# Routing stage of a one-core attention + mixture-of-experts kernel: constants, first rows and bias rows fetched during the attention stage, slots placed one iteration sooner, w2 two parts a step

## What is computed

```python
x = x + conv_ref(ln_c(x), w_qkv, b_qkv, rpb, w_proj, b_proj)     # attention ... out @ w_proj.T + b_proj
t = to_tokens(x)
# t + ffn(ln_t(t)):
gate_logits = xf @ Wg + bg
top_w, top_i = top_k(gate_logits, 2); top_w = softmax(top_w)
for e in range(E):
    h = gelu(xf @ W1[e] + b1[e], approximate=False)
    out = out + w_dense[:, e:e + 1] * (h @ W2[e] + b2[e])
```

## Time and profile before

| what | value |
|---|---|
| median of 3 executions | 1350.75 us (1346.7 to 1353.21) |
| the profiled execution | 1352.15 us, span 1350.3 us |
| busy, share of the span | PE 85%, PE weight load 72%, DVE 67%, POOL 55%, ACT 47% |
| last tile of the attention stage done | about 510 us after the span's start |
| first instructions of stage_c | 512.14 us |
| last send of stage_c issued | 685.31 us |
| first instruction of stage_e on POOL | 690.93 us |

### The profile page before, as it was taken

How to read it: one execution, slowest core, us unless ns; L and a number is a source line. 1 busy time by engine, 2 the same in 40 slices (tenths; PEclk the granted TensorE clock), 3 DMA queues, 4 the chain that set the end, 5 groups by cost and what they waited for, 6 DMA issues and landing times. The chain is left out here.

```text
span 1350.3 us, 38316 instructions
## 1 busy us (share of the span) xinstructions
PE 1143.8 (85%) x12145; PEld 967.9 (72%) x12146; DVE 907.0 (67%) x3154; ACT 630.7 (47%) x1305; POOL 737.9 (55%) x792
## 2 busy tenths in 40 slices
PE   2888855889988885998139999999999999999995
PEld 1655635888887884876028888888888888888884
DVE  6666645888888784887326666666666666666662
ACT  2555544888888783765113333333333333333331
POOL 5111123666666560577734666666566665666655
PEclk9899886999999996998569999999999999999998
DMA  6566648776767736999521323332232332323332
GB/s 166 154 210 210 197 152 196 191 186 180 185 179 183 194 115 190 350 356 304 187 75 26 49 47 50 48 48 48 44 52 47 49 48 45 50 48 48 48 49 28
DMA packets 152234, 169.85 MB, mean 126 GB/s; under 512 B 14334, under 2 KB 144014, under 8 KB 151766
## 3 DMA queue, kind: packets, MB, share of 16 engines
q1 hardware_dynamic: 114996, 131.54, 34.4%
q0 software_dynamic: 21920, 29.38, 13.2%
q10 hardware_dynamic: 15250, 8.11, 2.4%
HBM read 108.36 MB, written 65.49 MB: 129 GB/s over the span
## 5 line engine op out<-in xcount | busy, mean ns | idle before, releaser
L1523 ACT ACTIVATE e_gf<-e_ps_h,keep_b 128x256 f32<-128x256 f32 x448 | 211.8, 473 | 414.3 <-PE e_ps_h L1470 414.3
L1470 PE MATMUL e_ps_h<-e_xt,w1s 128*128 128x256 f16 x2688 | 323.2, 275 | 5.1 <-PEq L1462 3.8
L1470 PEld LDWEIGHTS e_ps_h<-e_xt,w1s 128*128 x2688 | 247.8, 98 | 73.5 <-issue 39.2
L1485 PE MATMUL e_ps_y<-w2s,e_g_hi 128*128 x1792 | 296.4, 273 | 0.0
L825 POOL TENSOR_TENSOR b_p<-b_s,b_p 128x392 f16<-128x392 f32 x196 | 182.6, 931 | 119.9 <-DVE b_p L723 116.0
L1485 PE MATMUL e_ps_y<-w2s,e_g_lo 128*128 x896 | 244.4, 273 | 0.0
L1423 POOL DMA_INDIRECT out<-e_y,e_xg x112 | 182.6, 1630 | 78.4 <-POOLq L1420 44.5
L1546 DVE TENSOR_TENSOR e_g_lo<-e_gf,e_g_hi 128x256 f16<-128x256 f32 x448 | 207.1, 462 | 15.5
L1485 PEld LDWEIGHTS e_ps_y<-w2s,e_g_hi 128*128 128x128 f16 x1792 | 172.9, 98 | 19.3
L780 ACT ACTIVATE b_s<-b_s,b_neg_max 128x196 f32<-128x196 f32 x392 | 158.3, 455 | 21.1 <-DVE b_neg_max L704 20.9
L1544 DVE CAST e_g_hi<-e_gf 128x256 f16<-128x256 f32 x448 | 145.7, 325 | 23.3 <-ACT e_gf L1523 23.3
(11 more groups left out here) (142 smaller groups left out, 1652.8 us busy)
## 6 DMA issues: line engine op xcount, KB each, us to landing
b_v<-v_rows SPq DMA_DIRECT2D x196, 99.5 KB
e_xg<-slots SPq DMA_DIRECT2D x56, 273.0 KB, 2.8
b_k<-qk_hi SPq DMA_DIRECT2D x56, 196.0 KB
a_w_in<-in_w SPq DMA_DIRECT2D x16, 512.0 KB, 3.7
c_w_in<-in_w SPq DMA_DIRECT2D x16, 512.0 KB, 9.6
v_rows<-a_v SPq DMA_DIRECT2D x14, 455.0 KB, 6.9
a_x<-in_x SPq DMA_DIRECT2D x14, 448.0 KB, 6.3
qk_hi<-a_o_hi SPq DMA_DIRECT2D x14, 448.0 KB, 4.4
```

The source lines that it names most:

```text
L1470: mm = pe.matmul(ps_h[:, hc % 4, 0:ST], w1s[:, bass.ds(e, 1), w, a:a + 128].rearrange("p a n -> p (a n)"), xt[:, s, :, 2 * p + k, :], star ...
L1485: mm = pe.matmul(ps_y[:, s, h * C:(h + 1) * C], g[:, s, hc, h * 128:(h + 1) * 128], w2s[:, bass.ds(e, 1), w, a:a + C].rearrange("p a n -> ...
L1523: act.activation(gf[:, hc % 4, :], ps_h[:, hc % 4, 0:ST], ACT.Gelu, bias=b1_sb[:, bass.ds(e * HC + hc, 1)], scale=1.0 / WSCALE).then_inc(g ...
```

## The change

- A new function `opening` makes the buffers for constants, weights, bias rows and first rows once, for stage_b and stage_c both. stage_b's SP issues the nine DMAs of constants and weights ahead of the second band, and the first two steps' attention and input rows in the middle of the last band. stage_b's DVE makes the bias rows after its last tile (`projection_bias`).
- In stage_c, `place(i - 1)` is in DVE's iteration i, behind `low_half(i - 1)`; `rank(i - 1)` on PE is ahead of `turn_xn(i)`.
- The w2 parts are two a step in steps 2 to 9 and none elsewhere. On ACT `high_w2` is behind `high_half`, as the last thing of an iteration.
- ACT begins with a square root on the constant `eps`; SP loads the first w2 parts behind the attention rows of steps 2 and 3.

```diff
@@ stage_b, SP
                             sp.wait_ge(v_free, n + 1)
+                            if r_next is None and n == COLS:
+                                for i in range(2):
+                                    sp.dma_start(op["a"][:, i, 0:SIZES[i]], token_rows(attn, i)).then_inc(op["a_in"][i], 16)
+                                    sp.dma_start(op["x"][:, i, 0:SIZES[i]], token_rows(x, i)).then_inc(op["x_in"][i], 16)
...
                 pair(0, 0, 1, QR - HALF)
+                sp.dma_start(op["b_f"][:, :], bproj.to_broadcast([128, C])).then_inc(op["b_ld"], 16)
+                sp.dma_start(op["id"][:, :], ident).then_inc(op["w_ld"], 16)
+                sp.dma_start(op["w_p"][:, :, :], wproj).then_inc(op["w_ld"], 16)
...
@@ stage_b, DVE
+                def projection_bias():
+                    b_f, b_part, b_rows, step = op["b_f"], op["b_part"], op["b_rows"], op["b_step"]
+                    dve.memset(b_rows[96:128, :], 0.0)
+                    dve.memset(op["even"][:, :], 1.0 / 32)
+                    dve.memset(op["eps"][:, :], 1e-5)
+                    dve.wait_ge(op["b_ld"], 16)
+                    for n in range(3):
+                        dve.tensor_copy(b_part[:, :], b_f[:, :]).then_inc(step, 1)
...
                 pair(row_offset(BANDS - 1), False, True)
+                projection_bias()
                 for t in range(COLS):
                     dve.wait_ge(stored[t], 32)
@@ stage_c
-        parts = [[i] if i < STEPS_C - 2 else [2 * i - 12, 2 * i - 11] for i in range(STEPS_C)]
+        parts = [[2 * i - 4, 2 * i - 3] if 2 <= i < 2 + E else [] for i in range(STEPS_C)]
...
-                load_a(0)
-                load_x(0)
-                load_a(1)
-                load_x(1)
-                sp.dma_start(w_g[:, :, :], wg).then_inc(g_ld, 16)
-                for p in range(2):
-                    load_w2(p)
                 for i in range(2):
                     sp.wait_ge(a_tr, i + 1)
                     load_a(i + 2)
+                for p in range(2):
+                    load_w2(p)
@@ stage_c, PE
                     if i + 1 < STEPS_C:
                         project(i + 1)
+                    if i:
+                        rank(i - 1)
                     turn_xn(i)
                     if i + 2 < STEPS_C:
                         turn_attention(i + 2)
-                    if i == 1:
-                        pe.wait_ge(k_in, 80)
-                    if i:
-                        rank(i - 1)
                     gate_logits(i)
@@ stage_c, ACT
-                act.dma_start(id_c[:, :], ident).then_inc(w_ld, 16)
...
-                act.wait_ge(ready, 1)
+                act.activation(sd[:, 0, 0:1], eps[:, :], ACT.Sqrt)
                 take_attention(0)
                 take_attention(1)
                 for i in range(STEPS_C):
                     roots(i)
                     normalise(i)
-                    for p in parts[i]:
-                        high_w2(p)
                     take_xn(i)
                     if i + 2 < STEPS_C:
                         take_attention(i + 2)
                     high_half(i)
+                    for p in parts[i]:
+                        high_w2(p)
@@ stage_c, DVE
-                bias_rows()
-                for i in range(STEPS_C + 2):
+                dve.memset(hot[:, :, :, :].rearrange("p s b e -> p (s b e)").bitcast(F32), 0.0).then_inc(ready, 1)
+                for i in range(STEPS_C + 1):
                     if i < STEPS_C:
                         residual(i)
-                    if i >= 2:
-                        place(i - 2)
-                    if i < STEPS_C:
                         scales(i)
-                    if 1 <= i <= STEPS_C:
+                    if i:
                         choose(i - 1)
                         low_half(i - 1)
+                        place(i - 1)
                     if i < STEPS_C:
                         for p in parts[i]:
                             low_w2(p)
```

More of the change, by code:

```diff
@@ L452, in _, with opening, sb, sem @@
                 step(1, True)
-def stage_b(nc, qk_hi, qk_lo, v_rows, bias, q_mask, k_mask, ident16, attn):
+def opening(nc, c):
+    def sb(name, shape, dt):
+        return c.enter_context(nc.sbuf_tensor("o_" + name, shape, dt))
+    def sem(name):
+        return c.enter_context(nc.semaphore("o_" + name))
+    return {
+        "id": sb("ident", [128, 128], F32),
+        "w_p": sb("w_p", [128, KC, C], F32),
+        "w_g": sb("w_g", [128, KC, E], F32),
+        "b_f": sb("b_f", [128, C], F32),
+        "b_part": sb("b_part", [128, C], BF16),
+        "b_rows": sb("b_rows", [128, C], BF16),
+        "even": sb("even", [128, 128], BF16),
+        "b_g": sb("b_g", [128, E], F32),
+        "eps": sb("eps", [128, 1], F32),
+        "cf": sb("consts", [128, C_CONSTS], F32),
+        "tri": sb("tri", [128, 2, 128], BF16),
+        "tok": sb("tok", [128, TOKENS // 128], I32),
+        "tc": sb("tiles", [1, T_CONSTS], F32),
+        "a": sb("a", [128, 2, GPS, C], F32),
+        "x": sb("x", [128, 2, GPS, C], F32),
+        "w_ld": sem("w_ld"), "b_ld": sem("b_ld"), "g_ld": sem("g_ld"), "k_in": sem("k_in"), "b_step": sem("b_step"),
+        "a_in": [sem(f"a_in{i}") for i in range(2)], "x_in": [sem(f"x_in{i}") for i in range(2)],
+    }
+def token_rows(t, i):
+    at = sum(SIZES[:i])
+    return t[at * 128:(at + SIZES[i]) * 128, :].rearrange("(g p) c -> p g c", p=128)
+def stage_b(nc, qk_hi, qk_lo, v_rows, bias, q_mask, k_mask, ident16, attn, x, wproj, bproj, wg, bg, ident, consts, tri,
+            tok_no, tiles, op):
     with ExitStack() as c:
@@ L832, in _, with stage_c @@
                 pair(False, True)
-def stage_c(nc, x, attn, wproj, bproj, wg, bg, ident, w2, consts, tri, tok_no, tiles, b1, b2, ident16, x1_out, slots_dram,
-            spare, carry, w2s, keep):
+def stage_c(nc, x, attn, w2, b1, b2, ident16, x1_out, slots_dram, spare, carry, w2s, keep, op):
     with ExitStack() as c:
@@ L900, in stage_c @@
         full_at = tc[0:1, E + 1 + NT:E + 1 + NT + MAXT]
[L902 to L905, removed]
+        w_ld, g_ld, k_in, a_in, x_in = (op[n] for n in ("w_ld", "g_ld", "k_in", "a_in", "x_in"))
         keep_in = sem("c_keep_in")
@@ L978, in _ @@
                     load_a(i + 2)
+                for p in range(2):
+                    load_w2(p)
                 for i in range(STEPS_C):
                     sp.wait_ge(add_ok, i + 1)
-                    sp.dma_start(rows(x1_out, i), x1[:, i % 2, 0:groups(i)]).then_inc(st_x1[i % 2], 16)
+                    sp.dma_start(token_rows(x1_out, i), x1[:, i % 2, 0:groups(i)]).then_inc(st_x1[i % 2], 16)
                     if i + 2 < STEPS_C:
@@ L1065, in _ @@
                 turn_attention(0)
-                pe.wait_ge(ready, 1)
                 project(0)
@@ L1069, in _ @@
                 pe.wait_ge(g_ld, 16)
+                pe.wait_ge(k_in, 80)
+                pe.wait_ge(ready, 1)
                 for i in range(STEPS_C):
@@ L1628, in program @@
                     qk_hi, qk_lo, v_rows, bias, w1s)
-            stage_b(nc, qk_hi, qk_lo, v_rows, bias, t["q_mask"], t["k_mask"], t["ident16"], attn)
+            stage_b(nc, qk_hi, qk_lo, v_rows, bias, t["q_mask"], t["k_mask"], t["ident16"], attn, t["x"], t["wproj"],
+                    t["bproj"], t["wg"], t["bg"], t["ident"], t["route"], t["tri"], t["tok_no"], t["tiles"], op)
         w2s = c.enter_context(nc.sbuf_tensor("w2s", [128, E, 2, EW], F16))
@@ L1634, in program @@
             ("tile_expert", [1, NT], I32), ("row_no", [1, NT], I32))}
-        stage_c(nc, t["x"], attn, t["wproj"], t["bproj"], t["wg"], t["bg"], t["ident"], t["w2"], t["route"], t["tri"],
-                t["tok_no"], t["tiles"], t["b1"], t["b2"], t["ident16"], out, slots, t["spare"], carry, w2s, keep)
+        stage_c(nc, t["x"], attn, t["w2"], t["b1"], t["b2"], t["ident16"], out, slots, t["spare"], carry, w2s, keep, op)
         stage_e(nc, slots, out, w1s, w2s, keep)
```

56 lines of the change are left out of this document (16 added, 40 removed).

## The result

| | before | after |
|---|---|---|
| median | 1350.11 us (1346.70 to 1353.21, 4 runs) | 1376.85 us (1375.48 to 1381.04, 4 runs) |
| span of the profiled execution | 1350.3 us | 1375.9 us |
| mean granted TensorE clock | 0.939 | 0.927 |
| routing stage: first instruction | 512.2 us | 519.94 us |
| its last send over | 686.3 us | 710.5 us |

The ratio is 1.0204, 95% interval 1.018 to 1.0228: slower by 26.7 us of medians. In the two profiles 24.2 us of it stand at the last send, and the first instruction of stage_e keeps its distance from that send (4.6 us before, 4.5 after). 7.7 of the 24.2 are there already when the routing stage begins.

The account below looks back on a forecast made before the run. The prediction took the chain through ACT and DVE, slowed by PE's lowered clock, to bound steps 2 to 9. Last send over at 531 + 122 + 56 = 709 against 686.3, 22.7 later than 1350.75: 1373 us, range 1355 to 1386.

Parts of the forecast that it names:

- Attention stage: Ahead of the routing stage: the 13 moved DMAs lengthen the attention stage by 0 us, bound 0 to 3.5.
- Start of the routing stage: With loads already on chip, step 2's residual add comes at 531 us instead of 536.66, 5.7 us gained.
- Full-clock step: Routing steps 2 to 9: the chain through ACT and DVE takes 13.1 us from residual add to residual add.
- Clock: PE pauses 4.2 us in each of eight steps, then about 5 us at 1.2 GHz: step 15.25 us (14.5 to 16.55).
- POOL: Routing steps 2 to 9: eight sends take 11.75 us, under 13.1, so POOL waits for slots 1.3 us each step.
- rival (b): Routing stage: POOL stays the bound if ACT and DVE finish a step in under 11.75 us; 1341 us, chance 0.08.
- Last stretch: From step 10's add to the end of the last send, with POOL's 36 sends behind again: 56.0 us.
- Rival (a): Routing steps: the clock stays up or recovers at once after PE's pauses, step 13.1 us; 1356 us, chance 0.15.
- Rival (c): Routing steps: w2 loads come late, each step grows by 2 us and the end by 16; 1389 us, chance 0.09.
- Rival (d): Routing stage's start gains nothing by the loads because PE or ACT waits for something else; 1379 us, no separate chance.

Follow-up runs that it names:

- filled: The changed kernel with 34 matmuls on constants, never read, in each of PE's eight pauses: 1365.94 us, ratio 1.0113.
- pair_early: The changed kernel with ACT's pair of high w2 parts back behind normalise, ahead of the copy out of PSUM: 1353.35 us, ratio 1.002.
- rows_later: one_early with the first token rows fetched at the start of the routing stage, not in the last band: 1351.49 us, ratio 1.0019.
- nine_tiny: buffers_only with nine 0.4 KB transfers on SP's queue ahead of the attention stage's band loop: 1373.72 us on the third chip, ratio 1.0045 to the kernel before.
- one_early: As pair_early, but with one w2 part a step: 1351.08 us, ratio 0.9998.
- constants_late: one_early with the nine constants issued in the last band, ahead of the rows: 1343.26 us, ratio 0.9945.
- buffers_only: The kernel before with the early buffers and semaphores reserved during stage_a and stage_b but unused: 1352.81 us, ratio 1.0017.
- w2_from_one: constants_late with w2 parts starting in step 1, two in each of the last three steps: 1364.71 us on the third chip, ratio 0.9976 to the kernel before.

## Why the prediction was right, step by step

The forecast was 1373 us (1355 to 1386), slower with a chance of 0.80. It came out at 1376.85. The mechanism was the one named, and filled and pair_early bear it out. That the number came so close is in part luck: several terms were off, and they nearly cancelled at the last send (forecast 709, measured 710.5; +7.7, -1.1, -6.1 and +1.0 in the list below).

- **Attention stage: forecast 0, bound 3.5; measured +6.6 us, and 1.1 more from ahead of it.** This step failed. The prediction took the 13 DMAs by their bytes and reasoned that "the loads are tiles ahead and SP waits for tiles". SP's rows before leave 2 us free in the 21.6 of half a band, and in rows_later 6.1 us of issuing put the next `b_k` 6.5 to 7.4 us back and the last one some 7. nine_tiny shows the same for 3.2 us with hardly a byte. About 0.7 us of the 6.6 is DVE's tail of bias rows: last reciprocal to stage start 4.42 us before, 5.11 after.
- **Start of the routing stage: forecast step 2's add 18.8 us into the stage; measured 17.7** (519.94 to 537.62). Right; 1.1 us sooner than worked out, inside its bounds.
- **Full-clock step: forecast 13.1; measured 13.24** in filled, in eight steps alike. The working on the two engines' queues holds to about 1%.
- **Clock: forecast 15.25 a step (14.5 to 16.55); measured 14.49**, the lower end: seven steps from 14.03 to 15.58 and the first of 13.25. The pause was 4.5 us (forecast 4.2). The mis-sized term is the low stretch, taken as 5 us: behind the pause that ended at 552.24 it was 3.1 us (a group of 1.30, then 1.03), behind the one that ended at 566.26 it was 5.8. It costs 1.25 us a step instead of 2.15. Eight steps: 6.1 us less than forecast.
- **POOL: forecast 11.75 us for eight sends, measured 10.1** (575.24 to 584.35 + 0.97). Sends that run while DVE stands still are not lengthened: a mean of 1003 ns against 1095. POOL so waits 4 to 5.5 us a step and not 1.3 to 3.5. Nothing hangs on it, as it is not the bound there, but the turning point of rival (b) was set too high at 11.75: a full queue took 11.1 us for eight sends already in the earlier trace rows, and 10.1 where DVE stands still.
- **Last stretch: forecast 56.0; measured 57.0** (653.52 to 710.47).
- **Rival (a)**, 1356 us at full clock: filled would be that kernel, and it took 1.0113 x 1350 = 1365. The rival had the full-clock step right and lacked the 7.7 us that are there when the routing stage begins.
- **Rival (b)**, POOL stays the bound, is what one_early and constants_late do; the order on ACT kept the changed kernel from it, as argued.
- **Rival (c)**, w2's loads late: not in the changed kernel (landing 5.3 us as a median, 9.6 before, as in long steps the DMA engines move 276 GB/s, the row above, and not the 380 of the earlier trace rows), but in pair_early, where DVE and ACT alone would allow a short step.
- **Rival (d)** falls: the start gained its 5.7 us and more.

In all: the place of the w2 parts costs 1.8% (24 us), of which the clock is about 12; the longer attention stage costs some 7 us, most of it by SP's queue, and takes back what the early fetches and the placing bring.

## What to carry to other kernels

Count the issues of a moved DMA as time on the queue that takes it, and read that queue's own timeline for gaps before calling it free; here 3.2 us of issues with 4 KB on a nearly full queue made the stage 5.3 us longer. The same two parts of w2 gave a ratio of 1.002 in ACT's wait for its neighbour and 1.0204 behind the last instruction of the iteration, where they were paid in the step and again in TensorE's clock. Of a bundle of edits, run each alone: here placing sooner (0.9969) and late-fetched constants (0.9945 together with it) were worth having, and the misplaced w2 parts and constants hid them.

## What the runs showed of the hardware

- The stretch at 1.2 GHz behind pauses of the same length, 4.5 us, was 3.1 us in one step and 5.8 in the next.
- A transfer of 0.4 KB held SP's queue for 0.37 us (2.93 us for eight, nine_tiny). In rows_later one of 256 KB (`o_w_p`) held it for 0.43 us, and one of 64 KB (`o_ident`) for 1.87: the issue times of these nine do not follow the sizes.
- The kernel before took 1349 to 1350 us on two chips and 1368 on a third. It was not profiled there, but nine_tiny and buffers_only have the same instructions in the routing stage, and it takes 190.7 us in the one on the third chip, 173.5 in the other on the second. Waits marked "remote" come in three of the four profiles of that chip; their cause stays open.
- Two profiles of the same attention stage code (constants_late and w2_from_one, on two chips) differ by 4.1 us, so a difference of that size in one profile needs the medians beside it.
